# Language-model tower on one core: last feed-forward chunk padded to 128 rows, TensorE's loop step rotated

## The reference

```
DIM, DEPTH, HEADS, DIM_HEAD, WINDOW, DIM_INNER = 256, 6, 16, 64, 64, 682
for i in range(DEPTH):
    x = attn_layer(shift_tokens(x), Wqkv[i], q_scale[i], k_scale[i], Wo[i]) + x
    x = ffn_layer(shift_tokens(x), ln_g[i], ln_b[i], W1[i], b1[i], W2[i], b2[i]) + x

def ffn_layer(x, g, bln, W1, b1, W2, b2):
    xn = (x - mu) / jnp.sqrt(var + 1e-05) * g + bln
    a, gate = jnp.split(xn @ W1 + b1, 2, -1)
    return a * jax.nn.gelu(gate, approximate=False) @ W2 + b2
```

## Time and profile before

| | |
|---|---|
| median of 3 runs | 4176.97 us (4171.86 to 4179.23) |
| the profiled execution | 4173.6 us, span 4171.8 us |
| mean granted TensorE clock | 0.975 |
| busy: PE, DVE, ACT, POOL | 96%, 71%, 63%, 50% of the span |
| local layers | from 1256.9 us to the end |

### The profile page before, as it was taken

One profiled execution on the slowest core, in us unless ns is written; L12 is line 12 of the kernel. 1 busy time (PEld: TensorE's weight loads), 2 busy tenths in 40 slices (PEclk: granted clock), 3 DMA queues, 4 the chain that ended last, 5 costly groups with the idle time before them and its releaser, 6 DMA issues.

```text
span 4171.8 us, 97939 instructions
## 1 busy us (share of the span) xinstructions
PE 3999.7 (96%) x33244; PEld 2841.6 (68%) x33244; DVE 2980.7 (71%) x5352; ACT 2635.9 (63%) x7072; POOL 2069.8 (50%) x1371
## 2 busy tenths in 40 slices
PE   6999988999678999999999999999999999999998
PEld 3666545665355777777777777777777777777777
DVE  4888547887787777777767776677767777777775
ACT  3677534777535676767666666767666666666665
POOL 1000001000137666666666666666666666666774
PEclk8999998999779999999999999999999999999999
DMA  6111132221103000110011100120011100111110
GB/s 161 37 44 42 25 113 68 55 53 32 61 19 116 21 19 21 59 45 19 21 41 44 38 19 22 51 53 22 19 30 51 42 19 21 53 50 23 23 26 24
DMA packets 103536, 177.53 MB, mean 43 GB/s; under 512 B 27541, under 2 KB 62129, under 8 KB 102961
## 3 DMA queue, kind: packets, MB, share of 16 engines
q1 hardware_dynamic: 102320, 169.70, 15.3%
q0 software_dynamic: 768, 2.10, 0.4%
HBM read 94.93 MB, written 23.07 MB: 28 GB/s over the span
## 4 chain that ended last, share of the span: by engine, by line
PE 68%; issue 1%; POOL 0%; DMA 0%; DVE 0%; ACT 0%; POOLq 0%; DVEq 0%; ACTq 0%; SPq 0%
PE PS L2281 23%; PE PS L2389 10%; PE PS L2367 8%; PE PS L2405 7%; PE PS L2356 5%; PE PS L2328 4%; PE PS L2337 4%; PE PS L2291 2%; PE PS L2301 2%; PE PS L2393 1%; PE PS L2376 1%; PE PS L2267 1%; PE PS L2323 0%; POOL rinv L2200 0%; POOL swp L2190 0%
## 5 line engine op out<-in xcount | busy, mean ns | idle before, releaser
L938 DVE TENSOR_REDUCE maxima<-PS 128x1 f32<-128x512 f32 x1024 | 632.4, 681 | 123.1 <-PE PS L772 122.7
L2226 POOL TENSOR_TENSOR probs<-probs,prob_recip 128x512 f32<-128x512 f32 x384 | 486.7, 1286 | 467.0 <-DVE prob_recip L2668 466.5
L2281 PE MATMUL PS<-wqk,xT 128*128 128x512 f32 x1536 | 711.0, 596 | 3.8 <-DMA wqk<-in_L_ffn_Wqkv 2.6
L2190 POOL TENSOR_TENSOR swp<-raw,table 128x512 f32<-128x512 f32 x384 | 651.7, 1708 | 0.7 <-DVE ss L2610 0.6
L902 ACT ACTIVATE probs<-PS 128x512 f32<-128x512 f32 x1024 | 520.0, 603 | 154.9 <-PE PS L786 154.2
L2539 ACT ACTIVATE probs<-probs,neg 128x128 f32<-128x128 f32 x1536 | 596.3, 402 | 1.3 <-DVE neg L2662 0.2
L2200 POOL TENSOR_TENSOR rinv<-ssm,power 128x32 f32<-128x32 f32 x96 | 531.4, 5535 | 66.9 <-DVE ssm L2617 66.7
L2281 PEld LDWEIGHTS PS<-wqk,xT 128*128 128x128 f32 x1536 | 286.3, 191 | 329.4 <-issue 324.4
L2389 PEld LDWEIGHTS PS<-xnT,w 128*128 128x128 f32 x3840 | 458.7, 192 | 45.7 <-issue 45.6
L2389 PE MATMUL PS<-xnT,w 128*128 128x128 f32 x3840 | 475.3, 275 | 0.9 <-issue 0.9
L772 PE MATMUL PS<-k_stack,q_stack 112*128 112x512 f32 (+1 forms) x1024 | 430.5, 442 | 35.6 <-PEq L640 18.9
(11 more groups left out here) (282 smaller groups left out, 7872.1 us busy)
## 6 DMA issues: line engine op xcount, KB each, us to landing
V_window<-V SPq DMA_DIRECT2D x180, 256.0 KB, 3.6
wqk<-in_L_ffn_Wqkv SPq DMA_DIRECT2D x12, 1024.0 KB, 5.2
w<-in_L_ffn_W SPq DMA_DIRECT2D x18, 640.0 KB
q_stack<-spin_qk SPq DMA_DIRECT2D x128, 80.0 KB
k_stack<-spin_qk SPq DMA_DIRECT2D x128, 80.0 KB
q_stack<-tok_qk SPq DMA_DIRECT2D x128, 64.0 KB, 2.7
k_stack<-tok_qk SPq DMA_DIRECT2D x128, 64.0 KB, 2.8
spin_qk<-shared SPq DMA_DIRECT2D x32, 256.0 KB
```

Of the source, the lines that this page charges most:

```text
L938: dve.tensor_reduce(maxima[:, k // 2, k % 2:k % 2 + 1], SM(r, k), AX.X, ALU.max).then_inc(sm_maxed, 1)
L2190: pool.tensor_tensor(swp[:, w, :, a:a + LD // 2], raw[:, w, :, b:b + LD // 2], table[:, j % 2, 2 + w, a:a + LD // 2].rearrange("p (o d) -> ...
L2226: pool.tensor_tensor(view, view, psr[:, 4 * q:4 * q + 4].rearrange("p (h o) -> p h o", o=1) .to_broadcast([P, 4, P]), ALU.mult).then_inc(p ...
L2281: mm = pe.matmul(wide(kind, half, j), xT[:, k, at:at + P], rhs, start=(k == 0), stop=(k == DC - 1))
```

## The change

Two things. (1) The last chunk of `hidden` and `w2` is cleared once, and `ffn_out` uses all 128 rows in every chunk. (2) TensorE's step begins with the second half of the queries; what stood ahead of it stands at the end of the step before, its lags lower by one. The three job lists are rotated to match. TensorE's first `ffn_in` and SyncE's load of the feed-forward weights wait for `cleared` to be 7.

```diff
-        W_JOBS = [("v", 0, 3), ("k", 1, 2), ("k", 0, 2), ("v", 1, 3), ("q", 1, 2), ("f", 2, 6), ...]
-        T_JOBS = [("xn", 0, 6), ("x", 0, 1), ("kt", 0, 3), ("p", 0, 4), ("kt", 1, 3), ...]
+        W_JOBS = [("q", 1, 2), ("f", 2, 6), ..., ("s", 3, 3), ("v", 0, 2), ("k", 1, 1), ("k", 0, 1), ("v", 1, 2)]
+        T_JOBS = [("kt", 0, 3), ..., ("o", 0, 4), ("o", 1, 4), ("xn", 0, 5), ("x", 0, 0)]
-        NARROW_JOBS = [("wo", 0, 5), ("w2", 0, 6)]
+        NARROW_JOBS = [("w2", 0, 6), ("wo", 0, 4)]
...
-                sp.wait_ge(S["cleared"], 5)
+                sp.wait_ge(S["cleared"], 7)
                 load_ffn_in(first)
...
                 pool.memset(kT[:, :, 4 * P - WINDOW:4 * P], 0.0).then_inc(S["cleared"], 1)
+                pool.memset(w2[:, W2C - 1, :], 0.0).then_inc(S["cleared"], 1)
+                pool.memset(hidden[:, :, W2C - 1, :], 0.0).then_inc(S["cleared"], 1)
...
                     pe.wait_ge(S["xn_taken"], n + 1)
+                    if isinstance(n, int) and n == 0:
+                        pe.wait_ge(S["cleared"], 7)
...
                     for f in range(W2C):
-                        rows = P if f < W2C - 1 else TAIL1
-                        mm = pe.matmul(FFN, hidden[0:rows, j % 2, f, :], w2[0:rows, f, :], start=(f == 0), ...)
+                        mm = pe.matmul(FFN, hidden[:, j % 2, f, :], w2[:, f, :], start=(f == 0), ...)
...
                 def step(t, i, l):
-                    if t6:
-                        transpose_xn(t6)
-                    if t1:
-                        transpose_x(t1)
-                    if t3:
-                        project(t3, "v", 0)
-                    if t2:
-                        project(t2, "k", 1)
-                    if t2:
-                        project(t2, "k", 0)
-                    if t5:
-                        project_out(t5)
-                    if t3:
-                        project(t3, "v", 1)
                     if t2:
                         project(t2, "q", 1)
...
                     if t6:
                         ffn_out(t6)
+                    if t5:
+                        transpose_xn(t5)
+                    if t0:
+                        transpose_x(t0)
+                    if t2:
+                        project(t2, "v", 0)
+                    if t1:
+                        project(t1, "k", 1)
+                    if t1:
+                        project(t1, "k", 0)
+                    if t4:
+                        project_out(t4)
+                    if t2:
+                        project(t2, "v", 1)
```

More of the change, by code:

```diff
@@ L1924, in local_layers @@
         own_shift, prev_shift = some("a_own_shift"), some("a_prev_shift")
-        W_JOBS = [("v", 0, 3), ("k", 1, 2), ("k", 0, 2), ("v", 1, 3), ("q", 1, 2), ("f", 2, 6), ("f", 0, 6), ("q", 0, 2), ("f", 1, 6), ("s", 0, 3), ("s", 2, 3), ("s", 1, 3), ("s", 3, 3)]
-        T_JOBS = [("xn", 0, 6), ("x", 0, 1), ("kt", 0, 3), ("p", 0, 4), ("kt", 1, 3), ("p", 1, 4), ("qt", 1, 3), ("qt", 0, 3), ("p", 2, 4), ("p", 3, 4), ("o", 0, 4), ("o", 1, 4)]
+        W_JOBS = [("q", 1, 2), ("f", 2, 6), ("f", 0, 6), ("q", 0, 2), ("f", 1, 6), ("s", 0, 3), ("s", 2, 3), ("s", 1, 3), ("s", 3, 3), ("v", 0, 2), ("k", 1, 1), ("k", 0, 1), ("v", 1, 2)]
+        T_JOBS = [("kt", 0, 3), ("p", 0, 4), ("kt", 1, 3), ("p", 1, 4), ("qt", 1, 3), ("qt", 0, 3), ("p", 2, 4), ("p", 3, 4), ("o", 0, 4), ("o", 1, 4), ("xn", 0, 5), ("x", 0, 0)]
         W_BANKS, T_BANKS = 4, 3
-        NARROW_JOBS = [("wo", 0, 5), ("w2", 0, 6)]
+        NARROW_JOBS = [("w2", 0, 6), ("wo", 0, 4)]
         TAKEN = {("q", 0): [q_taken[0]], ("q", 1): [q_taken[1]], ("k", 0): [k_taken[0]], ("k", 1): [k_taken[1]],
@@ L2403, in ffn_out @@
                     for f in range(W2C):
-                        rows = P if f < W2C - 1 else TAIL1
-                        mm = pe.matmul(FFN, hidden[0:rows, j % 2, f, :], w2[0:rows, f, :], start=(f == 0), stop=(f == W2C - 1),
+                        mm = pe.matmul(FFN, hidden[:, j % 2, f, :], w2[:, f, :], start=(f == 0), stop=(f == W2C - 1),
                                        skip_group_check=True)
@@ L2409, in step @@
                 def step(t, i, l):
-                    t1, t2, t3, t4, t5, t6 = (stage(t, i, l, lag) for lag in (1, 2, 3, 4, 5, 6))
-                    if t6:
-                        transpose_xn(t6)
-                    if t1:
-                        transpose_x(t1)
-                    if t3:
-                        project(t3, "v", 0)
-                    if t2:
-                        project(t2, "k", 1)
-                    if t2:
-                        project(t2, "k", 0)
-                    if t5:
-                        project_out(t5)
-                    if t3:
-                        project(t3, "v", 1)
+                    t0, t1, t2, t3, t4, t5, t6 = (stage(t, i, l, lag) for lag in (0, 1, 2, 3, 4, 5, 6))
                     if t2:
```

## The result

| | before | after |
|---|---|---|
| median of 4 runs each, side by side | 4175.77 us (4171.86 to 4179.23) | 4130.18 us (4125.62 to 4134.85) |
| ratio, with its 95% interval | | 0.9892 [0.9877, 0.9907] |
| the same two kernels again, in a later session | 4173.14 us | 4123.75 us (4121.86 to 4125.64), ratio 0.988 [0.9862, 0.9897] |
| profiled execution: time, span, clock | 4173.6, 4171.8, 0.975 | 4134.85, 4133.0, 0.973 |
| local layers, first transpose to the end | 2914.9 us | 2865.9 us |

The forecast was 4129.5. The two profiled executions differ by less than the layers do (38.8 us against 48.9), because the execution recorded for after entered the local layers at 1267.1 and not at 1256.9.

What follows compares the result with a forecast made beforehand. TensorE's own instruction spacing and the loop's jump were taken to bound the kernel. Padding 32 plus jump 15.5 gave 47.5 us off: 4173.6 to 4126.1 profiled, 4129.5 for the median, range 4121 to 4143.

Steps and rivals of the forecast that it cites:

- The bound: In the local layers TensorE's own instruction spacing and the loop's jump set the time; other engines have about 135 us free per layer.
- Padding: 32 us: Feed-forward output: full rows in the last chunk save 0.345 us a tile, 0.2 for the last six of 96 tiles.
- Rival A: Feed-forward output: the padding pays nothing, only the jump's 15.5 us are won, 4161 us; chance 0.06.
- The jump: 15.5 us: Layer loop's jump back: rotation hides the branch and the instruction-supply gap, saving 15.5 of 16.7 us.
- what was left over: At each jump in its new place: 0.4 us still lost, 1.2 us in all.
- the cover: At the new jump: 4.7 us of queued output projection and value half, against 4.3 to 4.6 us for branch and restart.
- ScalarE, allowed 0 to 1 us: Behind the jump: ScalarE's own branch makes its product for x barely in time; 0 to 1 us a jump allowed.
- rival B: Behind the jump: padding pays, but the second gap stays at a new place, some 4 us a jump, 4140; chance 0.12.
- The count: Second gap, at x behind the jump: loop starts about ten instructions before a 256-instruction packet's end; rotated, some 185 are left.
- Rival D: Inside the loop body: late instruction packets stall TensorE up to 2.6 us each, 4212 at eight places; chance 0.05.
- Small edits: Two more clearings on POOL, about 0.3 us each, ahead of the layers: cost nothing, without cover 0.6 us.
- The sum: Whole kernel: 32 + 15.5 = 47.5 us off, 4126.1 us profiled, 4129.5 us for the median.

Runs made afterwards that it cites:

- experiment 1: The kernel before with the padding alone (clearings, their waits, full rows), order as before: 4143.43 us, ratio 0.992.
- experiment 3: The kernel after with 96 rows in the sixth chunk in place of 128: 4123.31 us.
- experiment 4: The kernel after with 64 rows in the sixth chunk in place of 128: 4156.43 us.
- experiment 2: The rotation alone: the kernel after with 42 rows in the last chunk and nothing cleared: 4158.07 us, ratio 0.9959.
- experiment 5: The padding-only kernel of experiment 1 with 96 idle TensorE instructions ahead of the loop's start: 4128.31 us.
- experiment 6: The kernel after with 172 idle TensorE instructions, so the loop starts about ten instructions before a packet's end: 4123.40 us.
- experiment 8: The padded kernel with TensorE's step begun at the second half of `weigh`, some 58 instructions before a packet's end: 4150.55 us.

## Why the prediction was right

**The bound.** Right. TensorE's order and spacing were all there was: both parts cut its own time, and no wait on another engine took their place.

**Padding: 32 us.** Measured 32.5 by the layers, 31.5 by the times alone (experiment 1), and 32.4 on top of the rotation (2898.3 less 2865.9). The term per tile, 0.345 us, measured 0.34 in the step. Taking the whole of it, and not the lower end, was right. The wording under it failed: "the price of changing the number of active rows" would have made 96 rows dear, and they are free (experiment 3). What costs is passing between groups of 96 or 128 rows and groups of 64 or 42, 0.20 us and 0.145 for the two borders. The Trainium skill's *TensorEngine Tiling (Array Packing)*, Key Properties, says that a change of tiling mode drains the engine; the runs agree, and add the price and the border, between 64 and 96 rows. The Trainium skill's *TensorE: Matmul & The Clock Gate*, closing table, gives a matmul of few rows the time of a full one; experiment 4 agrees for the second of the two 64-row matmuls (0.376 us, a full one has 0.379), not for the first behind the border (0.480), and the group of twelve with the transposes behind it is 0.34 us longer. Rival A, built on that, is out.

**The jump: 15.5 us.** Measured 16.6 by the layers and 16.8 by the times (experiment 2), against 16.7 in all that the jump cost: nothing is left. The term that was mis-sized is what was left over: 0.4 us a jump, 1.2 in all, and it measured nothing. Its parts: the cover, 4.7 us by the prediction and 4.62 measured, was enough with 0.8 to spare at the first jump, since the branch in its new place takes only 3.5 to 3.8; ScalarE, allowed 0 to 1 us, was on time. The 1.58 us that the prediction found behind x and called half pace are the lower clock: granted 0.89, 0.79 and 0.88 in the 15 to 16 us from the three jumps of before on, and 1.00 at the same work in after; this part went with the gaps. That stalls would come back behind the jump (rival B) is not so with some 184 instructions left in the packet (seven were left before, and some 79 more are recorded ahead of the loop) nor with 164 (experiment 5), and is so with twelve (experiment 6).

**The count.** The second gap was put down to a packet's end about ten instructions behind the loop's start, worked out from 36 packets a layer. Experiment 5 takes that gap away, experiment 6 brings it back, and experiment 1 moves it by three instructions for three. Of all steps this was the one most open to a story, and it is the best shown.

**Rival D**, stalls inside the loop's body: none in the changed kernel. They do exist, far smaller than feared: experiment 5, with packets ending elsewhere, has two waits of 0.2 us in `weigh`, where the rival allowed up to 2.6, and its four passes lose about 1.4 us together. The one wait of after, 0.2 us in layer 0, came 2.4 us behind the request for an instruction packet and looks like the same thing. So the argument against D, that the steps drift over all positions in a packet and show no wait, was too strong, and that the rotation met none in the loop was not worked out ahead: it is in part luck. **Small edits**: nothing, as forecast; the wait for seven clearings was over 10 us early.

**The sum.** 47.5 forecast, 48.9 measured in the layers, 45.6 and 49.4 by the medians of the two sessions. The forecast of 4129.5 met 4130.18 partly by luck: the medians of the same kernel in two sessions lie 6.4 us apart.

## What to carry to other kernels

A hardware loop's jump has a place in the work, and the place can be chosen: rotate the body so that the branch falls under wide matmuls already queued (here 4.7 us of them against a branch of 3.3 to 4.1), and count where the loop's first instruction lies in its packet of 256, since with a dozen or fewer left a gap of 0.6 to 2.9 us follows each jump, with 58 left about 1 us, and with 164 or 184 none. A last chunk of 42 or 64 rows costs 0.34 us at its borders each time, one of 96 nothing (other counts were not run); clear the rest once and use the full array, or place it next to work that is narrow anyway. When a gap is seen, see whether it follows an operation or a count, by adding idle instructions.

## What was not expected of the hardware

**96 rows cost as much as 128**, 64 as much as 42 (experiments 3 and 4).

**The next packet is asked for late.** The DMA view of after from 2121 to 2130 us, in 40 slices of 0.225 us:

```profile
GB/s 0 0 0 0 0 0 0 73 0 0 0 0 0 0 0 0 0 0 0 0 0 0 73 0 0 0 0 0 0 0 18 23 20 23 23 20 23 21 261 221
...
q8 instruction: 2, 0.03, 1.5%
```

The two lone bursts are the two instruction packets. The first, in the slice from 2122.6, is the jump's target, and the branch ends at 2125.26. The second is asked for only then, in the slice from 2125.95, 0.7 us behind the branch's end, though it must follow. From the gaps it can be used 3.3 us behind the branch's end (before: branch over at 2114.84, x at 2118.14), and 2.9 to 3.6 us in the twelve such gaps of before and of experiments 1, 6 and 8. So the packet behind a jump's target was late in each of these kernels, whose loop starts 58 instructions or fewer ahead of a packet's end.

**The branch isn't always dear.** The attention's loop has some 1345 TensorE instructions in its body, by those recorded from one branch to the next; the layer loop has some 9130 and pays 3.3 to 4.1 us. The attention's, in after:

```profile
L714 PEldq COMPARE_BRANCH  x8: 76/210/239, 224.5 to 994.5; - x8
```

0.21 to 0.24 us, and 0.08 the two times that it isn't taken. The Trainium skill's *Runtime: NRT & Kernel Launch*, Instruction fetch mechanics, gives TensorE instruction memory for 2048 instructions; the two loops lie on either side of that, which fits. No loop of a size in between was run, so that the memory's size is the cause is argued and not shown.

**Open.** Why the same branch takes 3.3 us in one execution and 4.1 in another was not found: in its new place it takes 3.3 to 3.9, in the old one 3.7 to 4.1, and no experiment took that apart.
